# A four-batch attention layer's row maxima taken by half batches, their rows sent by ScalarE

## What is computed

```python
scores = jnp.einsum('bhqd,bhkd->bhqk', q, k) * scale
scores = jnp.where(causal, scores, -jnp.inf)
y_ar = jnp.einsum('bhqk,bhkd->bhqd', jax.nn.softmax(scores, axis=-1), v)
e = v[:, :, 1:, :] - y_ar[:, :, :-1, :]
...
ma = jnp.einsum('bhqd,bhkd->bhqk', qa, ka)      # causal, no softmax
y_ma = jnp.einsum('bhqk,bhkd->bhqd', ma, e)
...
out = merge(y_ar) @ w_proj.T + b_proj + (merge(y_ma) @ w_proj.T + b_proj)
```

## Time and profile before

| | us |
|---|---|
| three runs | 706.55, 709.92, 710.32 |
| their median | 709.92 |
| the profiled execution's own time | 705.89 |
| its span | 704.1 |
| prologue, from span's start to the first exponential | 117.2 |
| attention over four batches, first exponential to the last batch's copy of `y_ar` | 229.4 |
| the rest (feed-forward, experts, linear attention, experts) | 357 |

### The profile page before, as it was taken

The page is one execution under the profiler, slowest core; times in us unless marked ns, Lnnn a source line. Parts: engine busy times, 40 slices in busy tenths (PEclk is TensorE's granted clock), DMA queues, the critical chain, the costliest instruction groups (busy, mean ns, idle before and its releaser), DMA issues.

```text
span 704.1 us, 9924 instructions
## 1 busy us (share of the span) xinstructions
PE 506.5 (72%) x3706; PEld 323.5 (46%) x3706; DVE 365.7 (52%) x950; ACT 196.7 (28%) x278; POOL 181.9 (26%) x208
## 2 busy tenths in 40 slices
PE   1777775998899999988686639634788888735930
PEld 1654322445444544533475528522454655424920
DVE  4555482668667676820655412135778777330221
ACT  1454313451543245065235002112123111101200
POOL 8564360000101010010023350044402022031035
PEclk9999896999999999999999559956999999656975
DMA  7537877332633422060430021107652620001213
GB/s 267 210 117 244 266 246 197 120 99 62 139 101 89 126 80 80 29 159 15 134 106 16 19 64 49 38 27 178 186 149 54 190 70 16 1 16 52 61 41 101
DMA packets 61471, 74.16 MB, mean 105 GB/s; under 512 B 6772, under 2 KB 38128, under 8 KB 61168
## 3 DMA queue, kind: packets, MB, share of 16 engines
q1 hardware_dynamic: 59376, 69.34, 33.6%
q0 software_dynamic: 2048, 4.20, 2.1%
HBM read 42.97 MB, written 30.41 MB: 104 GB/s over the span
## 4 chain that ended last, share of the span: by engine, by line
PE 46%; DVE 17%; POOL 8%; SPq 8%; issue 8%; DMA 7%; ACT 5%; POOLq 0%; DVEq 0%; ACTq 0%
PE ps_accum L1379 21%; PE ps_pair L1379 15%; PE ps_turn L1379 5%; POOL xe_scr L574 3%; DMA sb_ring<-sb_qs 3%; SPq L358 2%; DVE sb_work L1133 2%; PE ps_turn L1387 2%; POOL sb_work L720 2%; POOL sb_rstd L558 2%; DVE sb_work L1271 2%; DVE sb_mpart L1059 1%; SPq L352 1%; DVE sb_stats L960 1%; DVE sb_values L969 1%
## 5 line engine op out<-in xcount | busy, mean ns | idle before, releaser
L812 ACT ACTIVATE sb_work<-ps_pair 128x1024 f32<-128x1024 f32 x80 | 80.3, 1026 | 50.7 <-PE ps_pair L1379 49.8
L1379 PE MATMUL ps_pair<-sb_ring,sb_xsets 128*128 128x512 f32 x160 | 64.6, 480 | 11.4 <-DMA sb_ring<-sb_qs 5.7
L1059 DVE TENSOR_REDUCE sb_mpart<-ps_turn 128x4 f32<-128x512 f32 x80 | 55.0, 687 | 31.2 <-PE ps_turn L1379 31.1
L1059 DVE TENSOR_REDUCE sb_mpart<-ps_accum 128x4 f32<-128x512 f32 x80 | 55.0, 688 | 19.2 <-PE ps_accum L1379 18.2
L1379 PE MATMUL ps_accum<-sb_work,sb_v_aug 128*32 128x128 f32 (+3 forms) x768 | 57.7, 394 | 0.3 <-ACT sb_work L812 0.3
L1379 PE MATMUL ps_turn<-sb_ring,sb_m_sets 128*128 128x512 f32 x80 | 39.5, 494 | 10.0 <-DVE sb_mpart L1059 9.8
L1379 PE MATMUL ps_accum<-sb_ring,sb_m_sets 128*128 128x512 f32 x80 | 41.8, 523 | 4.5 <-DVE sb_mpart L1059 3.9
L1379 PEld LDWEIGHTS ps_pair<-sb_ring,sb_xsets 128*128 128x128 f32 x160 | 30.7, 199 | 22.5 <-issue 10.7
L624 POOL TENSOR_TENSOR sb_e_pad<-sb_v_next,sb_y_ar 128x128 f32<-128x128 f32 x16 | 7.3, 457 | 127.2 <-DVE sb_y_ar L1103 127.2
L1271 DVE TENSOR_TENSOR sb_work<-ps_pair,sb_cst 128x1024 f32<-128x1024 f32 x32 | 37.5, 1214 | 2.2 <-PE ps_pair L1379 2.2
L1133 DVE TENSOR_TENSOR sb_work<-ps_pair,sb_cst 128x1024 f32<-128x1024 f32 x32 | 37.7, 1218 | 0.9
(11 more groups left out here) (242 smaller groups left out, 1002.2 us busy)
## 6 DMA issues: line engine op xcount, KB each, us to landing
sb_m_sets<-q_scr SPq DMA_DIRECT2D x16, 256.0 KB
sb_xsets<-k_scr SPq DMA_DIRECT2D x16, 256.0 KB
...
```

Source lines behind the costliest of these rows:

```text
L812: act.activation(banks[:, 2 * i:2 * i + 2], pair[u % 2][:], ACT.Exp, scale=SCALE).then_inc(s["exp_done"], 1)
L1059: dve.tensor_reduce(mpart[:, m // NPAIR, m % NPAIR, :], max_banks[m % 2][:].rearrange("p (h k) -> p h k", h=HL), AX.X, ALU.max).then_inc(s ...
L1379: return pe.matmul(dst, lhsT, rhs, start=start, stop=stop, skip_group_check=True)
```

## The change

The maxima are numbered through all batches (n = 0 to 159) and made in **halves** of a batch (two sets, 20 units; q = 0 to 7). Ahead of the first loop only the first half of batch 0 is made. In the first five steps of batch 0's loop its second half follows, four units a step. From there on every step makes two units, each set of steps one set of units: batch b's sets 1 to 3 make sets 0 to 2 of batch b+1, and set 0 of batch b+1 makes that batch's set 3. So the last batch's first five steps have maxima too, and its loop waits, as the others', for the projection of the batch before.

Each half has its own `max_of_tiles`, `max_turn` (8 rows, into `turn[0]`, which the turned answers use too) and `max_t`. They stand in the loop, at steps 5 and 15, no more behind it. `turn_answers` and `answers_divide` move from the second to the third step of a set; for sets 0 and 2 PE waits there for ACT's copy of the maxima. The rows are sent by ACT (`max_row` on its queue): one send behind the copy, the other behind the fifth exponential of an odd set.

In SP's list the exponential's two first sets of batch 0 come before the last two batches' queries and keys are kept, the rows are gone, `load_exp_set` stands ahead of `next_max_set` in each set, and for batch 0 a `next_max_set(2)` (wait for 30 units) stands ahead of `load_state(0)`.

GpSimd makes the errors first in place and then copies them to `e_pad`, and PE waits for that copy only ahead of its first answers with `e_pad`. Moved rows of the other engines follow from this. The diff, cut to its core:

```diff
+HALF = 2 * NPAIR
+UNITS = B * NS * NPAIR
+def max_units(b, u):
+    hs, i = u // NG_X, u % NG_X
+    if b == 0 and hs == 0:
+        return HALF + 4 * i, HALF + 4 * i + 2, HALF + 4 * i + 4
+    first = NPAIR * (NS * b + NS - 1 + hs)
+    if first >= UNITS:
+        return UNITS, UNITS, UNITS
+    at = (0, 2, 4, 6, 8, 10)
+    return first + at[i], first + at[i] + 1, first + at[i + 1]
+def max_turn_in(b, u):
+    if u == NG_X:
+        return 2 * b + 1
+    if u == 3 * NG_X and b + 1 < B:
+        return 2 * b + 2
+    return None
...
-            def next_max_set(b, hs):
-                hold(sp, s["smax_mm"], NM * b + NPAIR * (hs + 1))
-                if hs + 2 < NS:
-                    load_max_set(b, hs + 2)
-                elif b + 1 < B:
-                    load_max_set(b + 1, hs + 2 - NS)
-            def max_row(b, hs):
-                sp.dma_start(ring[3 * HD:3 * HD + 1, hs % 2].bitcast(F32),
-                             mT[HL * hs:HL * hs + HL].bitcast(F32)).then_inc(s[f"xset{hs % 2}"], 16)
+            def next_max_set(n):
+                hold(sp, s["smax_mm"], NPAIR * (n + 1))
+                if n + 2 < B * NS:
+                    load_max_set((n + 2) // NS, (n + 2) % NS)
...
             keep_features(1)
-            keep_values(3)
-            keep_softmax(2)
-            next_max_set(0, 0)
-            keep_features(2)
-            next_max_set(0, 1)
-            keep_softmax(3)
-            keep_features(3)
             hold(sp, s["ffn_h"], NF * B)
             for hs in range(2):
                 load_exp_set(0, hs)
+            keep_values(3)
+            keep_softmax(2)
+            next_max_set(0)
+            keep_features(2)
+            next_max_set(1)
+            keep_softmax(3)
+            keep_features(3)
             hold(sp, s["v_kept"], 16 * B)
             load_values(0)
-            for kept in ("q_kept", "k_kept"):
-                hold(sp, s[kept], 48 * B)
-            next_max_set(0, 2)
-            hold(sp, s["max_t_evac"], 1)
-            for hs in range(2):
-                max_row(0, hs)
-            next_max_set(0, 3)
-            for kept in ("mq_kept", "mk_kept"):
+            for kept in ("q_kept", "k_kept", "mq_kept", "mk_kept"):
                 hold(sp, s[kept], 48 * B)
             hold(sp, s["zeroed"], 7)
             for b in range(B):
+                if b == 0:
+                    next_max_set(2)
                 load_state(b)
                 if b + 1 < B:
                     load_values(b + 1)
                 for hs in range(NS):
-                    if b + 1 < B:
-                        next_max_set(b + 1, hs)
                     hold(sp, s["st_mm"], NX * b + NG_X * (hs + 1))
                     if hs + 2 < NS:
                         load_exp_set(b, hs + 2)
-                        max_row(b, hs + 2)
                     elif b + 1 < B:
                         load_exp_set(b + 1, hs + 2 - NS)
-                if b + 1 < B:
-                    hold(sp, s["max_t_evac"], b + 2)
-                    for hs in range(2):
-                        max_row(b + 1, hs)
+                    if NS * b + NS - 1 + hs < B * NS:
+                        next_max_set(NS * b + NS - 1 + hs)
...
-                pool.tensor_tensor(dst, value, answer, ALU.subtract).then_inc(s["err_pad"], 1)
                 pool.tensor_tensor(value, value, answer, ALU.subtract).then_inc(s["err"], 1)
+                pool.wait_ge(s["err"], NS * b + hs + 1)
+                pool.tensor_copy(dst, value).then_inc(s["err_pad"], 1)
...
-            def max_t(b):
-                act.wait_ge(s["max_t"], b + 1)
-                if b:
-                    act.wait_ge(s["xset0"], 192 * b)
-                    act.wait_ge(s["xset1"], 192 * b)
+            def max_t(q):
+                act.wait_ge(s["max_t"], q + 1)
+                if q >= 2:
+                    act.wait_ge(s["xset0"], 192 * (q // 2))
+                    act.wait_ge(s["xset1"], 192 * (q // 2))
                 else:
                     act.wait_ge(s["q_kept"], 48 * B)
-                act.copy(mT, turn[1][0:H, :]).then_inc(s["max_t_evac"], 1)
+                act.copy(mT[q % 2], turn[0][0:H // 2, :]).then_inc(s["max_t_evac"], 1)
+            def max_row(q, i):
+                act.wait_ge(s["max_t_evac"], q + 1)
+                act.dma_start(ring[3 * HD:3 * HD + 1, i].bitcast(F32),
+                              mT[q % 2][HL * i:HL * i + HL].bitcast(F32)).then_inc(s[f"xset{i}"], 16)
...
                         answers_out(b, hs - 1)
+                    if u and max_turn_in(b, u - 1) is not None:
+                        q = max_turn_in(b, u - 1)
+                        max_t(q)
+                        max_row(q, 0)
+                    if hs % 2 and i == NG_X - 1 and (hs == 1 or b + 1 < B):
+                        max_row(2 * b + 1 + hs // 2, 1)
                 answers_out(b, NS - 1)
-                if b + 1 < B:
-                    max_t(b + 1)
                 act.wait_ge(s["yar_mm"], b + 1)
...
             max_t(0)
+            for i in range(2):
+                max_row(0, i)
...
+                for u in range(NX):
+                    hs, i = u // NG_X, u % NG_X
+                    first, _, last = max_units(b, u)
+                    maxima(first, last)
+                    if b and u == 1:
                         moments(norm_first(B + b - 1), x[b - 1], (b - 1) % 2)
-                    maxima(b + 1, 4, 6)
-                    if b:
+                    if b and u == 2:
                         normalise(norm_first(B + b - 1), x[b - 1], xn_third[b - 1], (b - 1) % 2)
-                    for hs in range(NS):
-                        maxima(b + 1, at[hs], at[hs + 1])
-                        if hs < NS - 1:
-                            answers_divide(b, hs)
-                    max_of_tiles(b + 1)
-                else:
-                    norm(norm_first(B + b - 1), x[b - 1], xn_third[b - 1])
-                    for hs in range(NS - 1):
-                        answers_divide(b, hs)
+                    if u + 1 < NX and max_turn_in(b, u + 1) is not None:
+                        max_of_tiles(max_turn_in(b, u + 1))
...
+            def max_turn(q):
+                half = q % 2
+                if q and not half:
+                    pe.wait_ge(s["y_norm"], NS * (q // 2 - 1) + 2)
+                pe.wait_ge(s["smax_red"], (HALF + NT) * (q + 1))
                 for t in range(NT):
-                    last = pe.transpose(turn[1][0:H, t * P:(t + 1) * P], mneg[:, t, :], ident)
+                    last = pe.transpose(turn[0][0:H // 2, t * P:(t + 1) * P],
+                                        mneg[:, t, 2 * HL * half:2 * HL * (half + 1)], ident)
                 last.then_inc(s["max_t"], 1)
...
                 pe.wait_ge(s["v_aug"], b + 1)
-                if ahead and b:
+                if b:
                     pe.wait_ge(s["yar_evac"], b)
                     pe.wait_ge(s["attn_x"], b)
                 for u in range(NX):
                     hs, i = u // NG_X, u % NG_X
                     if u + 2 < NX:
                         scores(b, u + 2)
-                    if ahead:
-                        max_scores(b + 1, 2 * u, 2 * u + 1)
+                    first, middle, last = max_units(b, u)
+                    max_scores(first, middle)
                     for kt in range(NT):
                         if (DIAGONAL[kt] + NT - kt - 1) // 2 == i:
                             answers(b, hs, kt)
-                    if hs and i == 1:
+                    if hs and i == 2:
+                        if hs == 1:
+                            pe.wait_ge(s["max_t_evac"], 2 * b + 2)
+                        elif hs == 3 and ahead:
+                            pe.wait_ge(s["max_t_evac"], 2 * b + 3)
                         turn_answers(b, hs - 1)
-                    if ahead:
-                        max_scores(b + 1, 2 * u + 1, 2 * u + 2)
+                    max_scores(middle, last)
+                    if max_turn_in(b, u) is not None:
+                        max_turn(max_turn_in(b, u))
                 pe.wait_ge(s["exp_done"], NX * (b + 1))
                 pe.wait_ge(s["state_in"], 112 * b + 112)
                 ma_scores(b, 0)
                 turn_answers(b, NS - 1)
-                if ahead:
-                    max_turn(b + 1)
                 pe.wait_ge(s["ka_tok"], b + 1)
                 pe.wait_ge(s["err"], NS * b + NS)
-                pe.wait_ge(s["err_pad"], NS * b + NS)
                 pe.wait_ge(s["y_norm"], NS * b + NS)
...
+                    if t == 0:
+                        pe.wait_ge(s["err_pad"], NS * b + NS)
                     ma_answers(b, t)
                 if ahead:
-                    pe.wait_ge(s["max_t_evac"], b + 2)
+                    pe.wait_ge(s["smax_red"], (HALF + NT) * (2 * b + 3) + NPAIR)
                 turn_tiles(turn[1], y_ar).then_inc(s["yar_mm"], 1)
...
+            max_scores(12, 16)
             turn_keys(B - 2)
             pe.wait_ge(s["ka_tok"], B - 1)
```

(6 more changed lines are left out.)

74 lines of the change are left out of this document (37 added, 37 removed).

## The result

The changed kernel takes 722.17 us, the median of four runs (719.92 to 724.64), beside 708.23 us for the kernel before (706.21 to 710.32) on the same chip. The ratio is 1.0197, with a 95% interval of 1.014 to 1.0255: slower by 2%. The forecast was 711.3 us, and the range ended at 716.0, so both missed. The profiled execution is the slowest of the four, 724.64 us, with a span of 722.5; that of before had 705.89 and 704.1.

A forecast was written before the change was run, and what follows sets the result against it. It took TensorE to bound the loop, DVE the masks, and late maxima rows and SP's list the prologue's end. Terms -0.8, -0.2, -0.6 and +4.7 made +3.1 on 708.2: 711.3 us, range 706.5 to 716.0.

The forecast's parts named there:

- The prologue gains 8.8: Up to the first exponential: ACT's wait for the features kept comes last, 108.4 instead of 117.21 us, minus 8.8.
- The values, the rows of maxima in time: Prologue: rows of maxima landed by 104 us, values copied by 108.1, neither holding up the first exponential.
- rival of the late rows: Prologue: rows sent while DMA engines are full land at 111.6; total +9.4, 717.6 us; chance 5%.
- Batch 0's first set gives back 5.3: Batch 0's first set: ten more units of maxima cost 5.3 us, between TensorE's 3.3 and DVE's 6.7.
- SP's list takes most of the rest: Batch 0: state loads behind `next_max_set(2)` delay the third exponential set to 136.4; TensorE waits about 2.8 us; 0.8 left.
- The wait cools TensorE (22%): Batch 0's third set: idle TensorE returns at 1.2 GHz, costing 1.7 us; +4.8, 713.0 us; chance 22%.
- The loop from there: Loops behind the third set: net minus 0.2 us for the rest of batch 0, minus 0.3 each for batches 1, 2.
- The last batch pays 4.7: Last batch's first set: ten units of maxima make it like batch 2's, plus 4.7 us.
- Masks: "zero, up to 0.4 either way": Masks of each batch: changes hidden under DVE's work there, zero, up to 0.4 us either way.
- The sum: Whole kernel: -0.8 at the third set, -0.2 and -0.6 for batches 0 to 2, +4.7 last batch: +3.1 us.
- The errors: Masks: TensorE's running sum may start 0.45 us sooner, hidden under DVE's masks; zero, up to 0.4 either way.

The follow-up runs named there:

- kernel 5: Kernel before with batch 0's first two exponential sets loaded earlier in SP's list and the first two rows of maxima sent by ACT: 708.5 us, ratio 0.9999.
- experiment 1: Changed kernel with batch 0's state loads and batch 1's values ahead of `next_max_set(2)` in SP's list: 712.5 us, ratio 1.0037 to the kernel before.
- experiments 3 and 4: 3: changed kernel with the error's old order, 718.7 us, ratio 1.0148; 4: kernel before with only the error's new order, ratio 1.0018.

## Why the prediction was wrong, step by step

- **The prologue gains 8.8.** Right in mechanism: ACT's wait for the features kept is what came last. 7.1 measured. SP came to its list 1.3 us later than before (93.71 for 92.42). The earlier exponential sets aren't the reason: SP had been idle for 2.4 us ahead of 93.71, waiting for unit 20 as I had said, and in kernel 5, which has the same early sets, it came at 92.26. The second profile of the kernel before has 93.30, so the term lies within what executions differ.
- **The values, the rows of maxima in time** (rival of the late rows): right, sent at 101.55, read at 104.94, never waited for behind that.
- **Batch 0's first set gives back 5.3:** 5.3.
- **SP's list takes most of the rest.** The mechanism was right, and experiment 1 shows it; its size was the first miss. I had the third set there at 136.4 and a wait of 2.8. It was 141.15 and 5.66. The state's loads went at 123.63 and not at 120.9 (1.7 of that from the prologue), SP was blocked for 11.4 us and not 10.9, and from the first send of the third set to its reader it took 6.0 us and not 4.4: I had a landing of 2.5, and it was 4.1 behind the last send. Each term alone was off by 0.5 to 1.7, and all in the same direction.
- **The wait cools TensorE (22%).** This rival came true, at the point that it named: past the 2.9 us that the earlier trace rows showed without loss. Clock 0.50 behind 5.66 us of idle. Its price of 1.7 was too low: it stood on some 3.5 us at half pace, a term that no row showed, and here the half clock lasted some 5.6 us and cost 2.8 (experiment 1). Against the forecast it is 2.5: 0.7 in the third set's own scores and 1.8 in the rest of batch 0's loop, which took 1.6 more where I had -0.2.
- **The loop from there, batches 1 and 2:** -0.9 and -1.0 instead of -0.3 each. I suppose that the division behind a step without answers was worth more than I gave it; no run shows it.
- **The last batch pays 4.7:** first stage 14.72 as predicted, 5.1 with the rest.
- **Masks: "zero, up to 0.4 either way".** The second miss, and the larger one against its own bounds: +5.8. I had said of `max_turn` that "behind the loop the old one was hidden by DVE's masks, so its removal gives nothing". In time on the path that is so. But the four transposes were also work for TensorE in the middle of an idle stretch. Without them, and in the new error order, it idles for 1.26, 0.22 and 0.39 us, where before it was 1.06 and 0.40. In 21 of 25 masks without them the clock fell to 1.2 GHz for some 3.5 us. There 32 products of `e_pad` take 1.94 us instead of 1.08 (236.06 in the changed kernel, 228.98 before), and the masks are no longer VectorE's.
- **The sum** was +3.1, the ledger has +15.2. Of the 12.1 between them, 5.8 are the masks, 3.0 the third set's wait (2.7 predicted, 5.7 measured up to its scores), 2.5 the cold stretch behind it and 1.7 the prologue; the last batch adds 0.4, and batches 1 and 2 take back 1.3. The medians differ by 13.9. Part of the gap is that the kernel before had no long mask in its profile, while it loses 1.5 us a run there on average; the rest isn't accounted for.
- **The errors:** nothing gained, nothing lost at equal clock, as forecast (experiments 3 and 4). Whether their new order has a part in the clock's fall is open.

The chances said 45% slower and 47% same. What failed is the step that put the removed `max_turn` and the masks at nothing; behind it come the size of the third set's wait and of the cold stretch. What was lacking is a rival in which a removed cover, and not a new wait, lets the clock fall.
